# State-space stage of a sandwich kernel: one of two running sums of GpSimd handed to TensorE for part of the steps, softplus and gate tasks moved, decay factors in three PSUM banks

## The chip, the cores and the metric

One core of a Trainium2 chip runs the whole program. The metric is the device time of one execution in microseconds (us), median of three runs.

## The reference, cut to what matters

Two residual layers over 2 x 2048 tokens of width 256. The change touches only the first sublayer of the first layer, a Mamba block followed by a router:

```python
xm, z = jnp.split(x @ W_in.T, 2, axis=-1)          # x is RMS-normed
xc = silu(conv4(xm) + conv_b)
dt, Bm, Cm = jnp.split(xc @ W_xproj.T, [R, R + N], axis=-1)   # R = 64, N = 16
delta = softplus(dt @ W_dt.T + b_dt)
dA = exp(delta[..., None] * A)
dBx = delta[..., None] * Bm[:, :, None, :] * xc[..., None]
def step(h, t):                                     # over time, 16 states, 512 channels
    dA_t, dBx_t, C_t = t
    h = dA_t * h + dBx_t
    return (h, jnp.einsum('ben,bn->be', h, C_t))
y = (ys + D_skip * xc) * silu(z)
return y @ W_out.T
```

## The kernel before

The state-space stage is the function `mamba_phase`; routing, experts and the second layer follow it and are not touched. The work is cut into 8 **units**: two sequences (`hf` 0 and 1) times four blocks of 512 tokens, taken in turn, two units in one pass of a hardware loop (`NB` = 4 passes). A unit has 16 **steps** n = 0 to 15, one for each of the 16 states of the recurrence. The 512 channels lie on 128 partitions in four chunks c, and the 512 tokens are four tiles j of 128. All five engines run the steps, each in the order in which its program is written out, and meet at semaphores:

- **GpSimd (POOL)** at step n writes dBx of state n+1, as two `product` operations of 128x1024 (L396), and adds what ScalarE weighted for tiles 1 and 3 to the running sum `acc` (`add`, L408, 128x512). The order is product, add of tile 1, product, add of tile 3. At step 1 there is no addition (ScalarE starts the sum itself) but the small chain `front_power` (L373, L375). After step 13 stands `front_u` (L380), the product delta*xc of the next unit, and after step 14 `rms`, four small operations (L385 to L391).
- **VectorE (DVE)** scans state n in four chunks (`scan`, L779, 128x512), two chunks, then `summed` for tile 0 (L742: transposed state times C, added into `acc`), two chunks, then `summed` for tile 2. Between them lie the gating of y (steps 2 to 5), `softplus_fix`, `softplus_sub` and `softplus_add` (L683, L690, L697), two residual additions (L710), and statistics (L669, L716).
- **ScalarE (ACT)** at step n writes the decay factors exp(delta*A) of state n+1, one 128x512 chunk per PSUM bank (`factor`, L551; four banks `dA0` to `dA3`), and the weighted copies of tiles 1 and 3 (`weighted`, L565) into two buffers `part`. A factor of chunk c waits until the scan of chunk c of the state before has read that bank. Long tasks stand in two slots, MID_ACT and END_ACT, by step. `silus` (end of step 8) takes a table load, the silu of z (128x2048, L524), those of xc, and a load back.
- **TensorE (PE)** at step n transposes state n-1 into two banks `h_ps` (`turn`, L921, tiles 0, 1, then the tasks in EARLY, tiles 2, 3, then those in LATE). Tile 0 waits for VectorE to have read tile 2 before it, tile 1 for ScalarE to have read tile 3, and so on. The tasks are the projections of the next unit: `xc` (convolution as matmuls, L855), `dt` (L863), `d` (L868), `z` (L859), `o` (output, L874), the y of the unit before (L839, L841), the router `r` (L882). All data are float32.
- **SyncE (SP)** loads the B rows by DMA, three steps ahead.

Hence at step n the additions and transposes concern state n-1, the scan state n, the products and factors state n+1. The gate between GpSimd and TensorE is that a product of state n+1 needs all transposes of step n-2.

## Time and profile before

| | us |
|---|---|
| median of 3 runs | 2460.2 (2458.91 to 2461.51) |
| the profiled execution | 2457.92, of which span 2456.2 |
| period of one unit (GpSimd's `front_power` 222.34 to 352.02) | 129.68 |
| from step 1 of the first unit to step 1 of the last (92.63 to 1002.37) | 909.7 |

Busy over the whole span: TensorE 1920.1 us (78%), VectorE 1676.1 (68%), ScalarE 1185.9 (48%), GpSimd 1483.1 (60%). The stage ends at about 1150 us. Busy shares over the whole span say little here; what a change in the stage is worth is read within one unit. In the rows, L numbers are lines of the kernel; `a_dA`, `a_hs` and so on are its buffers with the stage's letter in front; "[3.42 <-ACT a_part L565]" means that the engine sat idle 3.42 us before this instruction, and that ScalarE's write of `part` ended it.

### The profile page before, as it was taken

What the parts mean: (1) busy time and instruction counts of PE and PEld (TensorE: products, weight loads), DVE (VectorE), ACT (ScalarE), POOL (GpSimd) and SP (SyncE); (2) the same over time, 40 slices, a digit from 0 to 9 for tenths busy, and PEclk for the clock granted to TensorE, in tenths of its full rate; (3) what the DMA queues carried; (4) which work ended last, traced back from release to release, by engine and by line L of the source; (5) the groups of instructions that cost most, each with busy time, mean ns of one, the idle gap of its engine ahead of it and who ended that gap; (6) DMA issues with size and microseconds to landing.
All of it is one profiled execution on the core that took longest, in us unless ns stands there. A gap on an engine that the chain in (4) does not pass through costs nothing. (4 is left out here: it accounts for less than half of the span.)

```text
span 2456.2 us, 35764 instructions
## 1 busy us (share of the span) xinstructions
PE 1920.1 (78%) x10252; PEld 1469.4 (60%) x10253; DVE 1676.1 (68%) x3193; ACT 1185.9 (48%) x2021; POOL 1483.1 (60%) x1118
## 2 busy tenths in 40 slices
PE   6787878796979787876599999907877784799970
PEld 2445454554555554644499999904655664699970
DVE  1789898989899898985644444436734897644438
ACT  2776767777777767773222222226632441111112
POOL 1799999898989898984133333335622420355532
PEclk9797979797989888887699999958987896799995
DMA  4111111111111010112411111142000014122226
GB/s 125 36 35 40 36 40 35 40 35 41 37 38 38 29 45 31 44 36 82 165 48 47 48 48 47 41 139 77 9 18 11 9 35 163 44 70 70 68 66 191
DMA packets 76781, 138.63 MB, mean 56 GB/s; under 512 B 10370, under 2 KB 47874, under 8 KB 75859
## 3 DMA queue, kind: packets, MB, share of 16 engines
q1 hardware_dynamic: 62994, 99.67, 12.3%
q0 software_dynamic: 13632, 37.24, 4.9%
q8 instruction: 56, 0.92, 0.2%
q14 instruction: 99, 0.80, 0.1%
HBM read 104.86 MB, written 32.01 MB: 56 GB/s over the span
## 5 line engine op out<-in xcount | busy, mean ns | idle before, releaser
L779 DVE TENSOR_TENSOR_SCAN a_hs<-a_dA,a_carry,a_hs 128x512 f32<-128x512 f32 x512 | 628.9, 1267 | 78.2 <-POOL a_hs L396 38.7
L396 POOL TENSOR_TENSOR a_hs<-a_u,a_b_bc 128x1024 f32<-128x1024 f32 x258 | 626.4, 2431 | 0.4
L921 PE MATMUL a_h_ps<-k_ident,a_hs 128*128 128x128 f32 x2064 | 326.6, 307 | 147.1 <-DVE a_acc L742 79.1
L921 PEld LDWEIGHTS a_h_ps<-k_ident,a_hs 128*128 128x128 f32 x2064 | 268.0, 158 | 270.8 <-DVE a_acc L742 75.5
L551 ACT ACTIVATE a_dA<-a_delta,a_a_neg 128x512 f32<-128x512 f32 x512 | 350.8, 688 | 31.2 <-DVE a_hs L779 29.3
L408 POOL TENSOR_TENSOR a_acc<-a_acc,a_part 128x512 f32<-128x512 f32 x242 | 317.7, 1313 | 59.7 <-ACT a_part L565 58.7
L565 ACT ACTIVATE a_part<-a_h_ps,a_c_tok 128x512 f32<-128x512 f32 x242 | 165.9, 686 | 193.6 <-PE a_h_ps L921 186.4
L1221 POOL DMA_INDIRECT expert_rows<-m0e_ys,k_pair x71 | 79.1, 1114 | 232.4 <-DVE m0e_ys L1277 217.9
L855 PE MATMUL a_fx<-a_hT,a_w_x 128*128 128x512 f32 x432 | 201.9, 599 | 2.2 <-ACT a_halo L487 1.4
L742 DVE SCALAR_TENSOR_TENSOR a_acc<-a_h_ps,a_c_tok,a_acc 128x512 f32<-128x512 f32 x242 | 176.1, 728 | 30.7 <-PE a_h_ps L921 30.7
L1287 DVE TENSOR_TENSOR m0e_hT<-m0e_gs,m0e_u 128x512 f32<-128x512 f32 x70 | 48.2, 689 | 190.9 <-ACT m0e_gs L1240 190.9
L1240 ACT ACTIVATE m0e_gs<-m0e_g 128x512 f32<-128x512 f32 x71 | 42.4, 597 | 269.6 <-PE m0e_u L1318 269.6
L1244 ACT ACTIVATE m1e_hT<-m1e_u 128x512 f32<-128x512 f32 x71 | 42.4, 597 | 226.3 <-PE m1e_u L1318 226.3
L1318 PE MATMUL m1e_u<-m1e_xT,m1e_wu 128*128 128x128 f32 x1136 | 140.2, 277 | 0.2 <-DVE m1e_wu L1271 0.2
L1318 PE MATMUL m0e_g<-m0e_xT,m0e_wg 128*128 128x128 f32 x1136 | 140.1, 277 | 0.0
L1267 DVE TENSOR_SCALAR m1e_xT<-m1e_x,k_ln_w,k_ln_b 128x128 f32<-128x128 f32 x142 | 51.8, 406 | 129.1 <-PE m1e_x L1306 129.0
L1318 PE MATMUL m0e_u<-m0e_xT,m0e_wu 128*128 128x128 f32 x1136 | 139.0, 276 | 0.0
L1328 PE MATMUL m0e_y<-m0w_down,m0e_hT 128*128 x568 | 134.5, 380 | 0.2 <-DVE m0e_ys L1277 0.2
L1318 PEld LDWEIGHTS m1e_u<-m1e_xT,m1e_wu 128*128 128x128 f32 x1136 | 134.1, 194 | 0.6 <-issue 0.5
L1318 PEld LDWEIGHTS m0e_g<-m0e_xT,m0e_wg 128*128 128x128 f32 x1136 | 134.2, 194 | 0.1
L1328 PE MATMUL m1e_y<-m1w_down,m1e_hT 128*128 x568 | 134.2, 379 | 0.0
L1221 POOL DMA_INDIRECT expert_rows<-m1e_ys,k_pair x71 | 70.0, 987 | 104.9 <-DVE m1e_ys L1277 89.0
(420 smaller groups left out, 3793.2 us busy)
## 6 DMA issues: line engine op xcount, KB each, us to landing
a_b_bc<-b_rows SPq DMA_DIRECT2D x132, 256.0 KB, 3.1
c_y<-expert_rows SPq DMA_DIRECT2D x16, 512.0 KB, 5.7
q_y<-expert_rows SPq DMA_DIRECT2D x16, 512.0 KB, 5.9
norm_rows<-a_x SPq DMA_DIRECT2D x9, 512.0 KB, 3.2
m0w_up<-in_m_up SPq DMA_DIRECT2D x1, 4096.0 KB, 12.5
m0w_gate<-in_m_gate SPq DMA_DIRECT2D x1, 4096.0 KB, 22.4
m0w_down<-in_m_down SPq DMA_DIRECT2D x1, 4096.0 KB, 31.9
c_xl<-in_L_attn_x SPq DMA_DIRECT2D x8, 512.0 KB, 3.5
```

The source lines that it names most:

```text
L396: pool.tensor_tensor(hs[n % NBUF][:, half, :], u[s][:, half, :], b_bc[:, n % NBUF:n % NBUF + 1, :].broadcast_to([P, 2, T]), ALU.mult).then ...
L408: pool.tensor_tensor(acc[s][:, j, :], acc[s][:, j, :], part[:, j // 2, :], ALU.add).then_inc(s_add, 1)
L551: act.activation(dA[c][:], delta[s][:, c, :], ACT.Exp, scale=a_neg[:, c, k:k + 1]).then_inc(s_da, 1)
L565: act.activation(to, hT_ps[j % 2][:], ACT.Copy, scale=c_tok[s][:, j, k:k + 1]).then_inc(s_part, 1)
L742: dve.scalar_tensor_tensor(out=acc[s][:, j, :], in0=hT_ps[j % 2][:], scalar=weight, in1=acc[s][:, j, :], op0=ALU.mult, op1=ALU.add).then_i ...
L779: dve.tensor_tensor_scan(hs[k][:, c, :], dA[c][:], hs[k][:, c, :], carry[:, hf, c, n:n + 1], ALU.mult, ALU.add).then_inc(s_scan, 1)
L855: last = pe.matmul(ps[:], w_x[:, q, d, k * P:(k + 1) * P], hT[:, d, q:q + T], start=q == 0 and d == 0, stop=q == KC - 1 and d == DC - 1)
L921: last = pe.transpose(hT_ps[j % 2][:, c * P:(c + 1) * P], hs[(n - 1) % NBUF][:, c, j * P:(j + 1) * P], ident[:])
L1221: pool.indirect_dma_start(io["expert_rows"], bass.IndirectOffsetOnAxis(ap=per.pair[:, s:s + 1], axis=0), ys[s % 2][:], None).then_inc(s_st ...
L1267: last = dve.tensor_scalar(xT[k][:, c, :], x_ps[:, c, :], scale[:, c:c + 1], shift[:, c:c + 1], ALU.mult, ALU.add)
L1318: last = pe.matmul(ps[k][:, f, :], w[k][:, c, f * P:(f + 1) * P], xT[k][:, c, :], start=c == 0, stop=c == DC - 1)
L1328: last = pe.matmul(y_ps[k][:], hT[k][:, c, :], w_down[:, c, bass.ds(e * D, D)], start=c == 0, stop=c == FC - 1)
```

## The change

- **Sum of tile 3.** For steps 9 to 15 and step 0 of the next unit, GpSimd no longer adds `part` of tile 3. TensorE adds it, as a matmul with the identity into a PSUM bank `sum` (`pile`), one step later, between transposes 1 and 2 (that of step 0 after transpose 3). At step 11 it adds what GpSimd had summed in steps 1 to 8 (`pile_acc`), and ScalarE copies the bank back at step 1 (`copy_sum`), before TensorE's first y task, which now waits for it. That is 9 matmuls for 8 additions in each unit.
- **Factors in three banks.** The bank comes from there: `dA` has three banks, used in turn. A factor now waits for the scan three chunks back, not four. `factor(n,3)` moves from the end of step n-1 to the start of step n, ahead of `weighted(n,1)`.
- **Tasks.** The silu of z goes from step 8 to a task of its own, `gates`, at the end of step 3. The `dt` projection is split over steps 9 and 10. Exponential, rounding and logarithm of the softplus each go half a step later. On VectorE `softplus_fix` goes from the middle to the end of step 12, `softplus_sub` from the end of step 12 to the middle of step 13, `softplus_add` from the middle to the end of step 13. `front_u` on GpSimd goes from after step 13 to after step 14.
- **RMS.** Three of the four small operations of `rms` go from GpSimd to VectorE as two. A buffer `part` is cleared in the prologue.

```diff
-        dA = [m.ps(f"dA{c}", [P, T]) for c in range(EC)]
+        RING = 3
+        dA = [m.ps(f"dA{c}", [P, T]) for c in range(RING)]
+        sum_ps = m.ps("sum", [P, ED])
+        last_y = dA + [sum_ps]
...
-                 11: ["d2", "d3"], 12: ["o0"], 13: ["z0"], 14: ["z3"], 15: ["r"]}
+                 10: ["dt.2", "dt.3"], 11: ["d2", "d3"], 12: ["o0"], 13: ["z0"], 14: ["z3"], 15: ["r"]}
...
-        MID_ACT = {1: ["norms"], 2: ["f1"], 10: ["dt"], 11: ["d2", "d3", "exp"], 13: ["z0"], 14: ["x1", "z2", "z3"]}
-        END_ACT = {0: ["moments"], 1: ["f0"], 4: ["xc0"], 5: ["own"], 6: ["xc1"], 7: ["xc2"], 8: ["silus"], 10: ["d0", "d1"],
-                   11: ["round", "ct"], 12: ["ln"], 13: ["z1"], 14: ["g0", "g1"], 15: ["rows"]}
+        MID_ACT = {1: ["norms"], 2: ["f1"], 10: ["dt"], 11: ["d2", "d3"], 12: ["round"], 13: ["z0", "ln"], 14: ["x1", "z2", "z3"]}
+        END_ACT = {0: ["moments"], 1: ["f0"], 3: ["gates"], 4: ["xc0"], 5: ["own"], 6: ["xc1"], 7: ["xc2"], 8: ["silus"], 10: ["d0", "d1"],
+                   11: ["exp", "ct"], 13: ["z1"], 14: ["g0", "g1"], 15: ["rows"]}
...
-        ND, NO, ADDS = len(ON), len(OFF), len(OFF) * (NS - 1)
+        LAST_ADD = 8
+        ADD_SEQ = [(0, 1)] + [(n, j) for n in range(2, NS) for j in OFF if j == 1 or n <= LAST_ADD]
+        PILE_SEQ = [(-1, 3), (0, 3)] + [(n, 3) for n in range(LAST_ADD + 1, NS - 1)]
+        PILE_SEQ.insert(4, ("acc", 3))
...
+        SLOT = [g % RING for g in range(NS * EC - 1)] + [1]
+
+        def slot(n, c):
+
+            return SLOT[(n * EC + c) % (NS * EC)]
+
+        def last_scan(n, c):
+
+            g = n * EC + c - 1
+            while SLOT[g % (NS * EC)] != slot(n, c):
+                g -= 1
+            return g
+
+        def piled(U, n):
+
+            return lin(U, PILES, PILE_SEQ.index((n, 3)) + 1)
...
+                pool.wait_ge(s_ms, nth)
...
-                        if n == 14:
-                            rms(tile0, lambda per_: lin(U, per_, per_))
-                        if n == NS - 3:
+                        if n == NS - 2:
                             pool.wait_ge(s_xc, lin(F, 1, 1))
                             pool.wait_ge(s_free[side("xc3")], count("xc3", U))
                             for q in range(2):
                                 front_u(F, 1 - hf, q)
+                        if n == 14:
+                            rms(tile0, lin(U, 1, 1))
             end = (0, 2 * NB, None)
...
-                act.wait_ge(s_scan, lin(U, NS * EC, (n - 1) * EC + c + 1 + SCANNED))
-                act.activation(dA[c][:], delta[s][:, c, :], ACT.Exp, scale=a_neg[:, c, k:k + 1]).then_inc(s_da, 1)
+                act.wait_ge(s_scan, lin(U, NS * EC, last_scan(n, c) + 1 + SCANNED))
+                act.activation(dA[slot(n, c)][:], delta[s][:, c, :], ACT.Exp, scale=a_neg[:, c, k:k + 1]).then_inc(s_da, 1)
+
+            def copy_sum(U, s):
+
+                act.wait_ge(s_sum, piled(U, 0))
+                act.activation(acc[s][:, 3, :], sum_ps[:], ACT.Copy).then_inc(s_sumc, 1)
 
             def weighted(U, n, j, s):
 
@@ -556,12 +581,16 @@
                     return
                 act.wait_ge(s_turn, turned(U, n, j))
                 k = (n - 1) % NS
+                to = part[:, j // 2, :]
                 if n == 1:
                     act.wait_ge(s_free[side("ct")], count("ct", before(U)))
                     to = acc[s][:, j, :]
+                elif j == 1:
+                    act.wait_ge(s_add, added_count(U, 0, 1) + -1 if n == 0 else added_count(U, n - 1 if n > 2 else 0, 1))
+                elif n == 2 or n == 0 or n > LAST_ADD + 1:
+                    act.wait_ge(s_sum, piled(U, n - 1 if n != 2 else 0))
                 else:
...
+                        factor(U, n, 3, hf)
                         weighted(U, n, 1, here)
+                        if n == 1:
+                            copy_sum(U, 1 - hf)
                         factor(U, n + 1, 0, there)
...
                         factor(U, n + 1, 2, there)
                         for name in END_ACT.get(n, []):
                             task(name)
-                        factor(U, n + 1, 3, there)
...
-                last.then_inc(s_mv2, 1)
+                link(last, padded=True)
+                link(dve.tensor_tensor(ms[:], mv2[:, :, 0], mv2[:, :, 0], ALU.mult))
+                dve.scalar_tensor_tensor(out=ms[:], in0=ms[:], scalar=EPS_RMS, in1=mv2[:, :, 1],
...
-                        if n == 12:
-                            softplus_fix(F, 1 - hf)
                         if n == 13:
-                            softplus_add(F, 1 - hf)
+                            softplus_sub(F, 1 - hf)
                         scan(2)
                         scan(3)
                         summed(U, n, 2, here)
                         summed(U, n, 3, here)
                         if n == 12:
-                            softplus_sub(F, 1 - hf)
+                            softplus_fix(F, 1 - hf)
                             dve.wait_ge(s_full["Y"], count("o0", U))
                             dve.wait_ge(s_xn, lin(U, 1, 1))
                             residual(0, fy, tile0).then_inc(s_free["Y"], 1)
+                        if n == 13:
+                            softplus_add(F, 1 - hf)
                         if n == 15:
                             dve.wait_ge(s_full["Y"], count("r", U))
...
+            def pile(U, n):
+
+                pe.wait_ge(s_part, part_count(U, n, 3))
+                if n == LAST_ADD + 1:
+                    pe.wait_ge(s_sumc, lin(U, 1, 1))
+                pe.matmul(sum_ps[:], ident[:], part[:, 1, :], start=n == LAST_ADD + 1, stop=n == 0).then_inc(s_sum, 1)
+
+            def pile_acc(U, s):
+
+                pe.wait_ge(s_add, added_count(U, LAST_ADD, 3))
+                pe.matmul(sum_ps[:], ident[:], acc[s][:, 3, :], start=False, stop=False).then_inc(s_sum, 1)
+
...
+                        if n == 0 or n > LAST_ADD + 1:
+                            pile(U, n - 1)
                         for name in EARLY.get(n, []):
                             task(name, U, F, 1 - hf)
                         turn(U, n, 2)
                         turn(U, n, 3)
+                        if n == 0:
+                            pile(U, 0)
+                        if n == LAST_ADD + 3:
+                            pile_acc(U, hf)
```

TensorE, the last transposes of step 9 to the first half of step 10, without the row numbers. The operand names are output<-inputs; `a_h_ps0` and `a_h_ps1` are the two transpose banks, L863/L900 is `dt`. Before:

```order
L863 MATMUL a_fy<-a_xc1,a_w_proj 96x512 x4
L915 REGISTER_ALU
L919 REGISTER_ALU
L921 MATMUL a_h_ps0<-k_ident,a_hs1 128x128 x4
L921 MATMUL a_h_ps1<-k_ident,a_hs1 128x128 x4
```

After:

```order
L900 MATMUL a_fy<-a_xc1,a_w_proj 96x512 x2
L953 REGISTER_ALU
L957 REGISTER_ALU
L959 MATMUL a_h_ps0<-k_ident,a_hs1 128x128 x4
L959 MATMUL a_h_ps1<-k_ident,a_hs1 128x128 x4
L967 MATMUL a_sum<-a_part,k_ident 128x512
L900 MATMUL a_fy<-a_xc1,a_w_proj 96x512 x2
```

Half of `dt` now stands behind the first transposes of step 10, with the first `pile` ahead of it.

VectorE, from `summed` of tile 0 of step 12 on. L683/L717 is `softplus_fix`, L690 is `softplus_sub`, L779/L816 the scans, L744 the first residual addition. Before:

```order
L742 SCALAR_TENSOR_TENSOR a_acc0<-a_h_ps0,a_c_tok0,a_acc0 128x512
L681 REGISTER_ALU
L683 SCALAR_TENSOR_TENSOR a_acc1<-a_acc1,a_u1 128x1024 x2
L777 REGISTER_ALU
L779 SCALAR_TENSOR_TENSOR a_hs0<-a_dA2,a_carry,a_hs0 128x512
L778 REGISTER_ALU
L779 SCALAR_TENSOR_TENSOR a_hs0<-a_dA3,a_carry,a_hs0 128x512
L733 REGISTER_ALU
L742 SCALAR_TENSOR_TENSOR a_acc0<-a_h_ps0,a_c_tok0,a_acc0 128x512
L689 REGISTER_ALU
L690 TENSOR_TENSOR a_delta1<-a_delta1,a_acc1 128x1024
```

After:

```order
L779 SCALAR_TENSOR_TENSOR a_acc0<-a_h_ps0,a_c_tok0,a_acc0 128x512
L814 REGISTER_ALU
L816 SCALAR_TENSOR_TENSOR a_hs0<-a_dA2,a_carry,a_hs0 128x512
L815 REGISTER_ALU
L816 SCALAR_TENSOR_TENSOR a_hs0<-a_dA0,a_carry,a_hs0 128x512
L770 REGISTER_ALU
L779 SCALAR_TENSOR_TENSOR a_acc0<-a_h_ps0,a_c_tok0,a_acc0 128x512
L715 REGISTER_ALU
L717 SCALAR_TENSOR_TENSOR a_acc1<-a_acc1,a_u1 128x1024 x2
L842 REGISTER_ALU
L744 ISA
L744 TENSOR_TENSOR k_hidden<-k_hidden,a_fy 128x512
```

The fix stands behind both scans and the second `summed` of the step, and the subtraction is no longer ahead of the residual addition.

ScalarE, the end of step 3 and the start of step 4. L551/L571 are factors, L565/L594 weighted copies, L542 is the silu of z. Before:

```order
L565 ACTIVATE a_part<-a_h_ps1,a_c_tok0 128x512
L550 REGISTER_ALU
L551 ACTIVATE a_dA2<-a_delta0,a_a_neg 128x512
L551 ACTIVATE a_dA3<-a_delta0,a_a_neg 128x512
L557 REGISTER_ALU
L563 REGISTER_ALU
L565 ACTIVATE a_part<-a_h_ps1,a_c_tok0 128x512
```

After:

```order
L594 ACTIVATE a_part<-a_h_ps1,a_c_tok0 128x512
L571 ACTIVATE a_dA0<-a_delta0,a_a_neg 128x512
L541 ISA
L541 REGISTER_ALU
L542 ACT_TABLE_LOAD
L542 ACTIVATE a_z0<-a_z0 128x2048
L570 REGISTER_ALU
L571 ACT_TABLE_LOAD
L571 ACTIVATE a_dA1<-a_delta0,a_a_neg 128x512
L582 REGISTER_ALU
L589 REGISTER_ALU
L594 ACTIVATE a_part<-a_h_ps1,a_c_tok0 128x512
```

Two table loads and the long silu now stand between a factor and the next, and ahead of the weighted copy of step 4.

## Rows read from the trace of the kernel before

**Rows 1.** Busy time by stretch: steps 1 to 8, 9 to 13, 14 to next step 1.
```profile
core 0: us, PE busy (x) PEld busy (x) DVE busy (x) ACT busy (x) POOL busy (x), PEclk, DMA share, GB/s
222.34:278.60 56.26, 52.90 (x242) 32.80 (x240) 51.30 (x53) 41.62 (x75) 56.16 (x34) 0.96 0.12 38
278.60:324.20 45.60, 33.80 (x130) 21.40 (x131) 38.05 (x34) 34.24 (x52) 38.37 (x21) 0.85 0.11 35
324.20:352.02 27.82, 17.09 (x88) 12.56 (x86) 25.52 (x43) 18.82 (x40) 27.49 (x20) 0.71 0.13 42
```
**Rows 2.** GpSimd in order of time: start, length, line, operation, idle before and its ender.
```profile
264.39 2.39 POOL L396 TENSOR_TENSOR a_hs<-a_u,a_b_bc 128x1024 f32<-128x1024 f32 x1
266.70 1.31 POOL L408 TENSOR_TENSOR a_acc<-a_acc,a_part 128x512 f32<-128x512 f32 x1
267.92 2.41 POOL L396 TENSOR_TENSOR a_hs<-a_u,a_b_bc 128x1024 f32<-128x1024 f32 x1
...
322.99 1.27 POOL L408 TENSOR_TENSOR a_acc<-a_acc,a_part 128x512 f32<-128x512 f32 x1 [3.42 <-ACT a_part L565]
324.21 4.69 POOL L380 TENSOR_TENSOR a_u<-a_delta,a_xc 128x1024 f32<-128x1024 f32 x2
...
336.90 1.02 POOL L391 TENSOR_TENSOR k_row_scale<-a_ms,a_halfneg 128x4 f32 x1 [0.17 <-POOL a_ms L389]
...
353.96 4.68 POOL L396 TENSOR_TENSOR a_hs<-a_u,a_b_bc 128x1024 f32<-128x1024 f32 x2
```
**Rows 3.** VectorE in order of time, step 9 to the next unit's step 2.
```profile
273.90 2.46 DVE L779 TENSOR_TENSOR_SCAN a_hs<-a_dA,a_carry,a_hs 128x512 f32<-128x512 f32 x2 [0.43 <-POOL a_hs L396]
...
280.54 1.28 DVE L779 TENSOR_TENSOR_SCAN a_hs<-a_dA,a_carry,a_hs 128x512 f32<-128x512 f32 x1 [1.80 <-ACT a_dA L551]
...
287.39 0.75 DVE L742 SCALAR_TENSOR_TENSOR a_acc<-a_h_ps,a_c_tok,a_acc 128x512 f32<-128x512 f32 x1 [2.56 <-PE a_h_ps L921]
...
300.46 1.28 DVE L779 TENSOR_TENSOR_SCAN a_hs<-a_dA,a_carry,a_hs 128x512 f32<-128x512 f32 x1 [2.10 <-ACT a_dA L551]
...
303.48 4.59 DVE L683 SCALAR_TENSOR_TENSOR a_acc<-a_acc,a_u 128x1024 f32<-128x1024 f32 x2 [1.09 <-ACT a_acc L539]
...
311.01 4.88 DVE L690 TENSOR_TENSOR a_delta<-a_delta,a_acc 128x1024 f32<-128x1024 f32 x2
...
341.44 2.46 DVE L779 TENSOR_TENSOR_SCAN a_hs<-a_dA,a_carry,a_hs 128x512 f32<-128x512 f32 x2 [2.21 <-issue]
...
356.35 2.46 DVE L779 TENSOR_TENSOR_SCAN a_hs<-a_dA,a_carry,a_hs 128x512 f32<-128x512 f32 x2 [1.07 <-POOL a_hs L396]
```
**Rows 4.** TensorE in order of time (a float32 matmul is two records).
```profile
250.61 3.60 PE L855 MATMUL a_fx<-a_hT,a_w_x 128*128 128x512 f32 x8
...
301.58 5.31 PE L874 MATMUL a_fy<-a_w_out,a_z 128*128 128x256 f32 x16
...
307.60 3.62 PE L874 MATMUL a_fx<-a_w_out,a_z 128*128 128x256 f32 x16
...
316.54 3.78 PE L859 MATMUL a_fy<-a_hT,a_w_z 128*128 128x512 f32 x4 [4.24 <-DVE k_hidden L710]
```
**Rows 5.** Busy time by stretch: steps 3 to 8, and steps 15 to 1 (columns as in Rows 1).
```profile
232.00:276.00 44.00, 43.47 (x195) 25.83 (x193) 41.76 (x43) 31.45 (x55) 44.00 (x26) 1.00 0.12 37
...
336.00:356.00 20.00, 11.66 (x44) 8.94 (x45) 17.02 (x26) 11.64 (x25) 19.57 (x16) 0.50 0.21 69
```
**Rows 6.** ScalarE in order of time: step 8's long task, step 1's `norms`.
```profile
272.88 1.28 ACT L524 ACT_TABLE_LOAD   x1
274.18 1.91 ACT L524 ACTIVATE a_z<-a_z 128x2048 f32<-128x2048 f32 x1
...
354.10 2.07 ACT L464 ACTIVATE a_hn<-k_hidden,a_nb,a_pw 128x256 f32 x4
```
**Rows 7.** VectorE in the prologue, GpSimd idle.
```profile
69.28 2.36 DVE L683 SCALAR_TENSOR_TENSOR a_acc<-a_acc,a_u 128x1024 f32<-128x1024 f32 x2 [53.51 <-ACT a_acc L539]
```
**Rows 8.** GpSimd's last addition of the state-space stage.
```profile
1126.76 1.26 POOL L408 TENSOR_TENSOR a_acc<-a_acc,a_part 128x512 f32<-128x512 f32 x1 [0.18 <-ACT a_part L565]
```

68 lines of the change are left out of this document (36 added, 32 removed).

## The prediction, made before the changed kernel was run

> **What bounds the kernel now.** I read first the busy time by stretch of one unit, 129.68 us long (a unit and a step are as defined with the kernel above). In steps 1 to 8 GpSimd is busy 56.16 of 56.26 us, and TensorE 52.90 at a clock of 0.96; in steps 9 to 13 no engine is full (VectorE 38.05 of 45.60); from step 14 to the next unit's step 1 GpSimd is full again, 27.49 of 27.82 [rows 1]. So the bound changes within a unit. Then GpSimd in order of time: it never idles from the `front_u` at 324.21 through the next unit's step 8. A product starts 2.31 us before the addition behind it, an addition 1.22 before the next product, so a step is 2 x (2.31 + 1.22) = 7.07 us [rows 2]. VectorE's own step is four scans of 1.2 (two take 2.46 [rows 3]) and two sums of 0.65 from start to start, 6.1 us, with 0.6 more in steps 2 to 5, where y is gated. Then VectorE in order of time, to see who is late where GpSimd isn't: a chain through ScalarE and TensorE. Between step 9's first scan (273.90) and the end of step 15's work (341.44 less the 2.21 of waiting, 339.23) it waits 0.45, 1.80, 2.56, 2.10 and 1.09, together 8.0 us of 65.3 [rows 3]. From there to step 2's first scan at 356.35 it takes 17.1 us, which GpSimd's chain sets.
>
> **The change, part by part, for one unit.** I follow each engine's queue from the rows' durations, with 0.1 us for a semaphore, over three stretches, and compare the moments at which VectorE begins step 9, step 0 and step 2.
>
> *GpSimd loses work.* Eight additions at 1.22 are 9.8 us, and three small operations of `rms`, on the engine that is full in two of three stretches. In the first stretch (steps 2 to 8) none goes, so 7.07 a step stays the pace there. TensorE needs 6.9 for these steps (a pair of transposes twice, and four matmuls of 128x512 at 0.86 to 0.9 each: 3.60 for four [rows 4]); it is busy 43.47 of 44 us at full clock [rows 5]. So even without GpSimd there would be little to win there, and a delay of TensorE would be paid.
>
> *Steps 9 to 15.* VectorE's work is 65.3 - 8.0 = 57.3 us, plus 0.5 for the two small operations of `rms` with their waits. I expect these waits:
> - Step 9: 0.45 for GpSimd as before. `silus` is shorter by z's 1.91 [rows 6], but starts one scan later, since the factor ahead of it now waits for the step's fourth scan: 1.0 instead of 1.80.
> - Step 10: only half of `dt` stands ahead of the transposes. The first sum waits 0.7 instead of 2.56, the second 0.5, since the other half of `dt` now stands ahead of it, and a `pile` with it.
> - Step 12: `exp` has left the place ahead of the factor, but d0 to d3 are late by the split `dt`: 1.3 instead of 2.10, then 0.9 for the fourth factor behind `exp`.
> - Step 12, o0: before, the fix (4.59 [rows 3]) lay on VectorE while TensorE ran o0. Now both scans and the second sum come first, and that sum's transposes stand behind o0, with a `pile` ahead of it: 1.0. The wait for the rounding (1.09) goes.
>
> The fix takes 2.36 us for both halves in the prologue, with GpSimd idle [rows 7], and 4.59 beside GpSimd's products; by my queue the products of the next states still run beside fix and subtraction, so I leave both at the price of before. The waits are 0.45 + 1.0 + 0.7 + 0.5 + 1.3 + 0.9 + 1.0 = 5.85 us, the stretch is 57.8 + 5.85 = 63.65: 1.65 us less. Nine `pile` matmuls at 0.86 (1.9 at half clock, 3.78 for two [rows 4]) otherwise fall where TensorE has room: it is busy 33.80 of 45.60 and 17.09 of 27.82 [rows 1].
>
> *Step 0 to step 2.* VectorE's own work is 7.85 (step 0 with its statistics) and 6.1: 13.95 us instead of 17.1, if GpSimd is not late. GpSimd's chain now starts from the addition of step 14: weighted copy, addition 1.2, product 2.3, `front_u` 4.7, power 1.0, product 2.3; the product for step 0 is there 13.0 us after step 14's first scan ends, and VectorE comes for it 13.4 after. Four tenths of room: VectorE sets the pace. That is 3.15 us more, together 4.8. At step 1 `copy_sum` (0.7, as a 128x512 copy) stands ahead of `norms` (2.07 [rows 6]) and step 2's second factor comes 0.8 late: 4.0 left.
>
> *Steps 2 to 8.* GpSimd enters ahead of VectorE and is then held twice by ScalarE. Its first addition of step 2 waits 1.2 for the weighted copy, which stands behind `norms` and a factor. In step 4 it waits 0.7 for `gates`: two table loads of 1.28 and 1.91 [rows 6] between the weighted copies. This stretch is bound by GpSimd, so it is paid where before it was part of one group in step 8; TensorE, held by the same copies, adds perhaps 0.3. The three banks cost nothing in an ordinary step: the factor's room is two scans and a sum, 3.0 us, less its 0.7. At the end of the stretch 4.0 + 0.9 (VectorE need not wait for GpSimd's first product) - 1.9 - 0.3 = 2.7; I take 3.0, since part of the 1.9 falls into each other.
>
> One sentence of the Trainium skill weighs against `gates`. The page "ScalarE: Activation LUTs" (section "What ACT_TABLE_LOAD costs") puts each switch of table at about 1.28 us plus a drain of 1.38, so the extra pair of switches would be 5.3 us and not 2.6. The rows show the load's 1.28 and the silu starting 1.30 after the start of the load [rows 6], without the drain; by the page the sum would be smaller by 2.7 us a unit.
>
> *The loop's turn.* After every second unit VectorE waits 2.21 us for nothing that the trace shows [rows 3]. Before, GpSimd's chain covered it (both kinds of unit last 129.7); now VectorE is the late one there, so at 3 of the 7 transitions about 2.1 of the 3.0 is not won.
>
> *Ends.* The first unit gains some 0.2, the last one its 1.65 of steps 9 to 15. At the very end, in place of an addition of 1.26 [rows 8], a `pile` (0.9 to 1.9) and a copy of 0.7 stand before the last y: 0.8 lost.
>
> **Sum.** 4 x 3.0 + 3 x 0.9 + 0.2 + 1.65 - 0.8 = 15.8 us. Against the profiled execution (2457.92, 2.3 below the median) that is 2442.2, against the median of 2460.2 it is 2444.4. I say **2444 us**. Bounds: if the new waits of steps 9 to 13 vanish (5.4) for all 8 units but TensorE's 6.9 a step still hold steps 2 to 8, about 40 us more could go, toward 2405; I hold that for unlikely, as each has a named cause. On the other side the half clock, below.
>
> **Rivals.**
> *(a) The relief arrives in full.* GpSimd with 9.8 us less runs further ahead, fix and subtraction meet it idle (2.2 and 2.4 less) and TensorE keeps full clock in steps 9 to 13. Then a unit gains 3.0 + 2.5: 2460 - 15.8 - 8 x 2.5 = 2424. For it: VectorE works only 51.3 + 38.1 + 25.5 = 114.9 of 129.7 us [rows 1]. Against it: by my queue GpSimd still writes the products of the next two states while the fix and the subtraction run.
> *(b) No gain: the three banks couple ScalarE to VectorE.* The factor of the next step's second chunk now waits for this step's third scan, and the weighted copy of tile 3 stands behind it. If this makes the copy late by 0.4 for GpSimd in each of the seven steps 2 to 8, 2.8 of the 3.0 us are gone: about 2459. For it: ScalarE, TensorE and GpSimd are all near full there. Against it: GpSimd waits for no copy in steps 2 to 8 now, so the copies have room.
> *(c) Slower: TensorE becomes the late engine from step 9 to 13.* In the stretch of steps 15 to 1 it runs at 0.50 of its clock, that is 1.2 of 2.4 GHz, after gaps of over 2 us [rows 5]; o0 took 5.31 after such a gap, o1 with the same work 3.62 [rows 4]. o0 is now uncovered, so half clock costs 1.7 there, 1.2 on the half of `dt`, and 1.0 on each of two `pile` ahead of transposes that are waited for: 4.9 a unit against 3.0, 1.9 slower, 2460 + 8 x 1.9 = 2475. It decides once the granted clock in steps 9 to 13 falls from 0.85 to under about 0.75.
> *(d) The table switches cost a drain at step 3 as well*, hidden in step 8 until now: 2.7 a unit on GpSimd's pace, 2444 + 22 = 2466. The page named above states such a drain.
>
> **Chances.** Forecast 0.52, (a) 0.20, (b) 0.14, (c) 0.10, (d) 0.04. A measurement of this kernel can tell about 0.2%, 5 us, from no change. Faster than 2455.3: the forecast and (a), 0.72. Within: (b), 0.14. Slower than 2465.1: (c) and (d), 0.14. The range for 8 in 10 takes in the forecast, (a) and (b): 2423 to 2462.
>
> **What will show it.** In the trace of the changed kernel the period from one `front_power` to the next should be 126 to 127 us inside a loop pass and about 129 across its turn. GpSimd should idle 8 to 10 us in steps 9 to 15, most of it for `part`. VectorE's waits for `dA` and the transposes should total about 6 us in a unit, with one behind o0. Step 4's first addition should wait for `part`. If instead VectorE waits for `part`'s chain in every one of steps 2 to 8, (b) holds; if the clock in steps 9 to 13 is under 0.75, (c); if GpSimd shows no idle time in steps 9 to 13, the relief was not delivered. My working is wrong first of all if a queue that I walked has one more wait, since 0.6 us in each unit is already 0.2%.

## The result: slower by 0.8%, and the profile after

The changed kernel takes **2478.6 us** (median of 4 runs, 2477.29 to 2480.15), against 2460.86 for the kernel before beside it (2458.91 to 2463.14). The ratio is 1.0077, 95% interval 1.0064 to 1.0089. 2444 us had been forecast, a gain of 16 us; it became a loss of 18. The profiled execution has a span of 2476.7 us, 20.5 above the one of before; the mean period from one `front_power` to the next is 132.6 us (92.0 to 1019.9), where it was 129.96.

The first view is the busy time of each engine in three stretches of the changed kernel. Columns: stretch, its length, busy time of TensorE's matmuls, its weight loads, VectorE, ScalarE and GpSimd, the granted clock, DMA share, GB/s. The stretches begin with the first scan of step 2, with the scan that answers to 273.90 of before, and with the end of step 15's work [rows 1, 3].

```profile
229.67:277.89 48.22, 45.87 (x215) 28.13 (x214) 45.30 (x47) 39.69 (x69) 46.04 (x27) 1.00 0.14 39
277.89:346.32 68.43, 50.81 (x222) 32.02 (x220) 62.90 (x64) 48.31 (x79) 53.66 (x27) 0.90 0.08 28
346.32:363.20 16.88, 12.05 (x44) 7.91 (x45) 13.69 (x21) 10.30 (x24) 12.36 (x8) 0.60 0.19 66
```

With before cut at the same instructions:

| | before | forecast | after |
|---|---|---|---|
| steps 2 to 8 | 47.2 | 49.0 (47.2 + 1.0, and 0.8 for `copy_sum`) | 48.2 |
| from step 9 to the end of step 15 | 65.3 | 63.65 | 68.4 (70.3 in the unit before) |
| from there to step 2, inside a pass | 17.1 | 13.95 | 13.8 |
| the same across the loop's turn | 17.1 | 16.05 (13.95 + 2.1) | 17.0 |

Three of the four rows came out within 1 us of the walk: the third to 0.2 us, steps 2 to 8 0.8 us shorter and the loop's turn 1 us longer. The loss is in the second one. So the next view is VectorE in order of time over that stretch, of the changed kernel (start, length, engine, line, operation, out<-in, count, and in brackets the idle time before and what ended it).

```profile
283.43 1.28 DVE L816 TENSOR_TENSOR_SCAN a_hs<-a_dA,a_carry,a_hs 128x512 f32<-128x512 f32 x1 [0.70 <-ACT a_dA L571]
...
288.59 0.75 DVE L779 SCALAR_TENSOR_TENSOR a_acc<-a_h_ps,a_c_tok,a_acc 128x512 f32<-128x512 f32 x1 [0.87 <-PE a_h_ps L959]
...
292.04 0.75 DVE L779 SCALAR_TENSOR_TENSOR a_acc<-a_h_ps,a_c_tok,a_acc 128x512 f32<-128x512 f32 x1 [0.34 <-PE a_h_ps L959]
...
298.77 0.75 DVE L779 SCALAR_TENSOR_TENSOR a_acc<-a_h_ps,a_c_tok,a_acc 128x512 f32<-128x512 f32 x1 [0.51 <-PE a_h_ps L959]
...
301.16 1.28 DVE L816 TENSOR_TENSOR_SCAN a_hs<-a_dA,a_carry,a_hs 128x512 f32<-128x512 f32 x1 [0.45 <-ACT a_dA L571]
...
304.87 1.28 DVE L816 TENSOR_TENSOR_SCAN a_hs<-a_dA,a_carry,a_hs 128x512 f32<-128x512 f32 x1 [0.59 <-ACT a_dA L571]
307.23 0.75 DVE L779 SCALAR_TENSOR_TENSOR a_acc<-a_h_ps,a_c_tok,a_acc 128x512 f32<-128x512 f32 x1 [1.08 <-PE a_h_ps L959]
307.98 5.58 DVE L717 SCALAR_TENSOR_TENSOR a_acc<-a_acc,a_u 128x1024 f32<-128x1024 f32 x2
...
332.59 1.78 DVE L757 TENSOR_TENSOR a_ms<-a_mv 128x4 f32<-128x4 f32 x1
...
334.41 2.26 DVE L758 SCALAR_TENSOR_TENSOR a_ms<-a_ms,a_mv 128x4 f32<-128x4 f32 x1
...
345.47 0.75 DVE L779 SCALAR_TENSOR_TENSOR a_acc<-a_h_ps,a_c_tok,a_acc 128x512 f32<-128x512 f32 x1 [0.41 <-PE a_h_ps L959]
...
349.19 2.46 DVE L816 TENSOR_TENSOR_SCAN a_hs<-a_dA,a_carry,a_hs 128x512 f32<-128x512 f32 x2 [2.87 <-issue]
```

With the 0.45 before them, the waits up to 307.23 are 4.99 us; 5.85 had been forecast for the stretch. What was not forecast are durations. `softplus_fix` takes 5.58 us (4.59 before [rows 3]), and the two small RMS operations, of 128x4 elements, take 1.78 and 2.26 us and were put down at 0.5 together.

What GpSimd does at those moments, in the same kernel:

```profile
306.83 5.66 POOL L414 TENSOR_TENSOR a_hs<-a_u,a_b_bc 128x1024 f32<-128x1024 f32 x2
...
332.00 2.36 POOL L414 TENSOR_TENSOR a_hs<-a_u,a_b_bc 128x1024 f32<-128x1024 f32 x1
334.30 4.65 POOL L404 TENSOR_TENSOR a_u<-a_delta,a_xc 128x1024 f32<-128x1024 f32 x2
```

The first small operation, begun at 332.59, ends at 334.37; GpSimd's product ends at 334.36. The second ends at 336.67, when the first of the two `front_u` operations (4.65 for both) is over. All 8 units are alike in this; the ninth execution stands behind the loop. The view of all executions of one line gives minimum, median and maximum in ns:

```profile
L757 DVE TENSOR_TENSOR a_ms<-a_mv x9: 157/1498/1790, 200.2 to 1170.9; 128x4 f32<-128x4 f32 x9
```

```profile
L758 DVE SCALAR_TENSOR_TENSOR a_ms<-a_ms,a_mv x9: 164/2261/2265, 201.8 to 1171.1; 128x4 f32<-128x4 f32 x9
```

The minimum, 157 and 164 ns, is that of the execution behind the loop, where no `front_u` follows and GpSimd is idle. The second consequence lies on TensorE. In time order, first TensorE in the first unit of a pass, then VectorE:

```profile
207.16 1.97 PE L959 MATMUL a_h_ps<-k_ident,a_hs 128*128 128x128 f32 x8 [5.60 <-DVE a_acc L779]
...
210.62 3.42 PE L919 MATMUL a_fy<-a_w_router,a_acc 128*128 128x8 f32 x16
```

```profile
215.03 0.75 DVE L779 SCALAR_TENSOR_TENSOR a_acc<-a_h_ps,a_c_tok,a_acc 128x512 f32<-128x512 f32 x1 [2.63 <-PE a_h_ps L959]
```

TensorE idles 5.60 us while VectorE stands in the two operations, and then takes 3.42 us for the router. That is the lower of its two clock levels: the same router takes 1.85 at the upper one, as below. VectorE pays with a wait of 2.63 us for transposes, at a place where it had none. Not every unit goes this way. The next one has a longer gap, and the router runs at the upper level:

```profile
339.81 1.97 PE L959 MATMUL a_h_ps<-k_ident,a_hs 128*128 128x128 f32 x8 [5.88 <-DVE a_acc L779]
...
343.10 1.85 PE L919 MATMUL a_fy<-a_w_router,a_acc 128*128 128x8 f32 x16
```

In this trace the router takes 3.42 us in four of the eight units (2.6 us of waiting each on VectorE) and 1.85 to 1.87 in the other four (0.3 to 0.6 each), after gaps of 5.6 to 5.9 us in all eight. Together VectorE waits 12.3 us at this place.

### The profile page after: what moved, and what is told of

Its sections match the earlier page's. It is cut to its first block and busy times, and to the rows that moved or that the text cites. A ratio compares the mean times of both kernels' runs of the same rounds, so it can differ in the third digit from the quotient of the medians.

```text
span 2476.7 us, 35927 instructions
## 1 busy us (share of the span) xinstructions
PE 1944.3 (79%) x10402; PEld 1468.3 (59%) x10403; DVE 1720.4 (69%) x3220; ACT 1210.6 (49%) x2045; POOL 1397.8 (56%) x1026
## 5 line engine op out<-in xcount | busy, mean ns | idle before, releaser
L816 DVE TENSOR_TENSOR_SCAN a_hs<-a_dA,a_carry,a_hs 128x512 f32<-128x512 f32 x512 | 631.9, 1268 | 53.2 <-POOL a_hs L414 26.2
L571 ACT ACTIVATE a_dA<-a_delta,a_a_neg 128x512 f32<-128x512 f32 x512 | 352.8, 689 | 206.7 <-DVE a_hs L816 205.3
L959 PEld LDWEIGHTS a_h_ps<-k_ident,a_hs 128*128 128x128 f32 x2064 | 262.2, 154 | 278.3 <-DVE a_hs L816 95.2
L959 PE MATMUL a_h_ps<-k_ident,a_hs 128*128 128x128 f32 x2064 | 314.6, 297 | 141.4 <-DVE a_acc L779 100.2
L426 POOL TENSOR_TENSOR a_acc<-a_acc,a_part 128x512 f32<-128x512 f32 x177 | 227.9, 1288 | 158.4 <-ACT a_part L594 158.4
L779 DVE SCALAR_TENSOR_TENSOR a_acc<-a_h_ps,a_c_tok,a_acc 128x512 f32<-128x512 f32 x242 | 176.8, 730 | 40.3 <-PE a_h_ps L959 40.1
L594 ACT ACTIVATE a_part<-a_h_ps,a_c_tok 128x512 f32<-128x512 f32 x242 | 164.0, 678 | 45.6 <-PE a_h_ps L959 45.1
L1348 DVE TENSOR_TENSOR m0e_hT<-m0e_gs,m0e_u 128x512 f32<-128x512 f32 x70 | 48.2, 688 | 190.5 <-ACT m0e_gs L1301 190.5
L1379 PE MATMUL m0e_u<-m0e_xT,m0e_wu 128*128 128x128 f32 x1136 | 138.6, 275 | 0.0
L1379 PEld LDWEIGHTS m0e_u<-m0e_xT,m0e_wu 128*128 128x128 f32 x1136 | 132.8, 192 | 0.0
```

The lines of the kernel that those rows point to most:

```text
L426: pool.tensor_tensor(acc[s][:, j, :], acc[s][:, j, :], part[:, j // 2, :], ALU.add).then_inc(s_add, 1)
L571: act.activation(dA[slot(n, c)][:], delta[s][:, c, :], ACT.Exp, scale=a_neg[:, c, k:k + 1]).then_inc(s_da, 1)
L594: act.activation(to, hT_ps[j % 2][:], ACT.Copy, scale=c_tok[s][:, j, k:k + 1]).then_inc(s_part, 1)
L779: dve.scalar_tensor_tensor(out=acc[s][:, j, :], in0=hT_ps[j % 2][:], scalar=weight, in1=acc[s][:, j, :], op0=ALU.mult, op1=ALU.add).then_i ...
L816: dve.tensor_tensor_scan(hs[k][:, c, :], dA[slot(n, c)][:], hs[k][:, c, :], carry[:, hf, c, n:n + 1], ALU.mult, ALU.add).then_inc(s_scan, 1)
L959: last = pe.transpose(hT_ps[j % 2][:, c * P:(c + 1) * P], hs[(n - 1) % NBUF][:, c, j * P:(j + 1) * P], ident[:])
```

## The experiments

Each median stands beside a median of the kernel before on the same chip. Since the kernel before took 2457.15 to 2461.48 us in these groups, kernels of different groups are compared by their ratios to it; a difference of ratios is turned into us with 2460.

Two theories came first. **L**: the small operations on VectorE wait for GpSimd's running operation, and that, with what follows, is the loss. **T**: the loss comes from the rest of the change (three banks, `gates`, matmuls that add, softplus order).

**1. The small RMS operations back on GpSimd, all else as changed.**

```diff
+                pool.tensor_tensor(ms[:], mv2[:, :, 0], mv2[:, :, 0], ALU.mult).then_inc(s_ms, 1)
+                pool.tensor_tensor(ms[:], ms[:], eps_rms[:], ALU.add).then_inc(s_ms, 1)
+                pool.tensor_tensor(ms[:], ms[:], mv2[:, :, 1], ALU.add).then_inc(s_ms, 1)
...
-                link(dve.tensor_tensor(ms[:], mv2[:, :, 0], mv2[:, :, 0], ALU.mult))
-                dve.scalar_tensor_tensor(out=ms[:], in0=ms[:], scalar=EPS_RMS, in1=mv2[:, :, 1],
```

> The changed kernel with one part undone: the three small RMS operations (square of the mean, eps, variance, 128x4) are again GpSimd's, not two of VectorE's. Theory L (lock): in the changed kernel these two VectorE operations read two SBUF operands each and took 1.64 and 2.26 us on average where they took 0.16 each at the very end, with GpSimd idle, because each waits for the GpSimd operation that runs; that is 3.7 us a unit on VectorE, which is the late engine there, 29 us in all, and the TensorE clock that falls in the gap behind it. It expects 2446 to 2453 us, and VectorE's step 14 to be some 4 us shorter. Theory T (TensorE): the loss is from the sum on TensorE and the uncovered output projection at step 12. It expects 2474 to 2480 us, since nothing of that changes.

Measured: 2438.37 us (2436.87 to 2445.53), ratio 0.9932 (0.9912 to 0.9952). L holds and T falls: without this one part the change is a gain of 17 us, more than L's 2446 to 2453 us had allowed for. Beside number 10, which differs from it by less than the intervals, it is the fastest kernel of the study. GpSimd does the same work in three operations of 0.2 us each. TensorE there, in the first unit of a pass:

```profile
204.56 1.09 PE L965 MATMUL a_h_ps<-k_ident,a_hs 128*128 128x128 f32 x8 [1.74 <-DVE a_acc L785]
...
206.35 1.85 PE L925 MATMUL a_fy<-a_w_router,a_acc 128*128 128x8 f32 x16
```

The gap is 1.74 us and not 5.60, and the router takes 1.85. What VectorE does at the end of that unit:

```profile
211.90 2.46 DVE L822 TENSOR_TENSOR_SCAN a_hs<-a_dA,a_carry,a_hs 128x512 f32<-128x512 f32 x2 [1.35 <-POOL a_hs L423]
```

Here it waits 1.35 us for GpSimd's product at step 0. So not all that the two operations cost comes back: VectorE comes 4 us sooner, and GpSimd does the three small operations again ahead of that product.

**2. The same operations on VectorE, but ahead of step 14's scans.**

```diff
                         dve.wait_ge(s_carry, lin(U, NS, n + 2))
+                        if n == 14:
+                            dve.wait_ge(s_free["X"], count("o1", U))
+                            rms_stats(tile0, lin(U, 1, 1))
...
                         scan(0)
...
-                        if n == 14:
-                            dve.wait_ge(s_free["X"], count("o1", U))
-                            rms_stats(tile0, lin(U, 1, 1))
```

> The changed kernel with the same instructions, but VectorE's statistics and the two small RMS operations stand ahead of the scans of step 14, not between its two pairs of scans. There GpSimd sat idle for 5.8 to 6.1 us, waiting for a weighted copy that itself waits for the first scan. Theory L: each of the two operations takes 0.16 to 0.2 us, and the time is 2446 to 2453 us. Theory T: 2474 to 2480 us. If the two operations are slow by their own nature on VectorE (small tiles, dependence), they keep 1.6 and 2.3 us and the time stays at 2478 too.

Measured: 2451.01 us (2446.42 to 2457.97), ratio 0.9976 (0.9962 to 0.9989). All executions of the first small operation, and then GpSimd's waits between 90 and 1150 us (total, times, longest):

```profile
L757 DVE TENSOR_TENSOR a_ms<-a_mv x9: 156/158/158, 196.1 to 1140.4; 128x4 f32<-128x4 f32 x9
```

```profile
POOL a_acc L426 <- ACT a_part L594: 138.6, 48, 8.3
```

At a moment when GpSimd idles (from 191.23 to 199.22 in the unit where it stands at 196.09), the same instruction takes 0.158 us, and so in every unit. That is theory L in one line: operands, engine and code are the same, and what runs on GpSimd differs. The kernel is still 11 us behind number 1. A likely cause is that the statistics now stand ahead of the scans, and with them everything that GpSimd's chain waits for (its waits are 138.6 us, and 118.3 in number 1); this was not tested by itself.

**3. The kernel before with the small operations on VectorE alone.**

```diff
-                pool.tensor_tensor(ms[:], mv2[:, :, 0], mv2[:, :, 0], ALU.mult).then_inc(s_ms, 1)
...
+                link(dve.tensor_tensor(ms[:], mv2[:, :, 0], mv2[:, :, 0], ALU.mult))
```

> The kernel before with only one part of the change: the three small RMS operations of GpSimd become two of VectorE. Theory L: they take 1 to 2.4 us each here too, since GpSimd is always busy there, but VectorE had 3.3 us of waiting for GpSimd between this place and step 2, and GpSimd is relieved of 0.96 us: 2453 to 2464 us, so the same two operations that cost 29 us in the changed kernel cost nothing here. Theory T: 0.2 us each, 2452 to 2460 us; the durations tell the two apart, not the time.

Measured: 2471.33 us (2470.5 to 2474.75), ratio 1.0055 (1.0038 to 1.0072): slower, above what I had expected. VectorE, then GpSimd:

```profile
200.63 1.01 DVE L717 TENSOR_TENSOR a_ms<-a_mv 128x4 f32<-128x4 f32 x1
...
201.68 1.19 DVE L718 SCALAR_TENSOR_TENSOR a_ms<-a_ms,a_mv 128x4 f32<-128x4 f32 x1
...
212.17 0.75 DVE L739 SCALAR_TENSOR_TENSOR a_acc<-a_h_ps,a_c_tok,a_acc 128x512 f32<-128x512 f32 x1 [0.92 <-PE a_h_ps L918]
```

```profile
199.26 2.36 POOL L390 TENSOR_TENSOR a_hs<-a_u,a_b_bc 128x1024 f32<-128x1024 f32 x1
201.58 1.26 POOL L402 TENSOR_TENSOR a_acc<-a_acc,a_part 128x512 f32<-128x512 f32 x1
```

The first operation ends at 201.64 and the product at 201.62; the second at 202.87 and the addition at 202.84. Here they cost 2.2 us and not 4.0, since a short addition stands behind the product and not `front_u`. What I had missed is that the transposes are late behind them here too: 0.92 behind a router of 3.42 us, and 1.34 at 230.46, behind matmuls for y most of which also ran at the lower clock. The router takes 3.42 us in all eight units here, and in four of eight in the kernel before.

**4. The changed kernel with z's silu back in step 8.**

```diff
-                act.activation(z[s][:], z[s][:], ACT.Silu).then_inc(s_zc, 1)
...
+                act.activation(z[1 - s][:], z[1 - s][:], ACT.Silu).then_inc(s_zc, 1)
```

> The changed kernel with the silu of z back in the long task at the end of step 8 (one pair of table loads a unit, not two). If a table switch costs a drain or the task at step 3 holds GpSimd's chain by more than the 1.0 us for which its addition waits in the trace, the time falls by 10 us or more, to under 2469. By the prediction's own step (0.7 us of GpSimd's time won at step 4, but the long task at step 8 1.9 us longer, with VectorE waiting for it) it stays within 2472 to 2486.

Measured: 2493.2 us (2490.99 to 2494.87), ratio 1.0145 (1.0128 to 1.0162). So the move of `gates` is worth 17 us, in spite of its extra pair of table loads. One row of VectorE shows why:

```profile
285.08 1.28 DVE L817 TENSOR_TENSOR_SCAN a_hs<-a_dA,a_carry,a_hs 128x512 f32<-128x512 f32 x1 [2.49 <-ACT a_dA L572]
```

With three banks, VectorE waits 2.49 us for a factor behind the full `silus`, and 0.70 without z's part. 1.8 us in each of 8 units are 14 us, and over the stage VectorE's waits for factors rise by 11.5 (29.9 for 18.4); what the rest of the 17 us is was not traced. The time lies above the whole range expected: the prediction's step had `gates` about neutral.

**5. The kernel before with three banks alone** (slots, waits and the fourth factor's place at the start of the next step as in the change; no other part of it).

```diff
-                act.wait_ge(s_scan, lin(U, NS * EC, (n - 1) * EC + c + 1 + SCANNED))
+                act.wait_ge(s_scan, lin(U, NS * EC, last_scan(n, c) + 1 + SCANNED))
```

> The kernel before with one part of the change alone: the decay factors use three PSUM banks in turn (the fourth lies unused), the fourth factor stands at the start of the next step. By the prediction's step (room of 3.0 us for a factor in an ordinary step, a little lost at the long tasks of steps 8 and 11) the time is 0 to 8 us above before, ratio 1.000 to 1.003. Rival (b), ScalarE coupled to VectorE in every step, expects 16 us or more above, ratio 1.007 and up.

Measured: 2506.98 us (2503.51 to 2511.7), ratio 1.0192 (1.0175 to 1.0209), 47 us slower: the largest effect of the study, and "the three banks cost nothing in an ordinary step" had been my line. VectorE, then GpSimd:

```profile
287.69 1.28 DVE L793 TENSOR_TENSOR_SCAN a_hs<-a_dA,a_carry,a_hs 128x512 f32<-128x512 f32 x1 [2.49 <-ACT a_dA L565]
...
295.69 0.75 DVE L756 SCALAR_TENSOR_TENSOR a_acc<-a_h_ps,a_c_tok,a_acc 128x512 f32<-128x512 f32 x1 [3.71 <-PE a_h_ps L935]
...
319.31 5.39 DVE L704 TENSOR_TENSOR a_delta<-a_delta,a_acc 128x1024 f32<-128x1024 f32 x2
...
328.83 4.79 DVE L711 TENSOR_TENSOR a_delta<-a_delta,a_u 128x1024 f32<-128x1024 f32 x2
```

```profile
327.98 1.27 POOL L422 TENSOR_TENSOR a_acc<-a_acc,a_part 128x512 f32<-128x512 f32 x1 [4.36 <-ACT a_part L579]
329.21 3.33 POOL L410 TENSOR_TENSOR a_hs<-a_u,a_b_bc 128x1024 f32<-128x1024 f32 x1
```

In steps 2 to 8 VectorE has no wait that before had not, so the line is right as it stands; the time is in the range that rival (b) had claimed, but not by its mechanism. But each long task meets VectorE with one scan less in hand: 2.49 for 1.80, 3.71 for 2.56 [rows 3]. After the subtraction the chain goes on: ScalarE waits for a scan behind the long VectorE operations, its weighted copy comes 4.36 us late for GpSimd, GpSimd's product (3.33) now runs beside `softplus_add`, and this takes 4.79 us where it took 2.35.

**6. Twice the adding matmuls.** Number 1 with each of the 8 matmuls that add `part` issued twice.

```diff
-                pe.matmul(sum_ps[:], ident[:], part[:, 1, :], start=n == LAST_ADD + 1, stop=n == 0).then_inc(s_sum, 1)
+                pe.matmul(sum_ps[:], ident[:], part[:, 1, :], start=n == LAST_ADD + 1, stop=False)
+                pe.matmul(sum_ps[:], ident[:], part[:, 1, :], start=False, stop=n == 0).then_inc(s_sum, 1)
```

> The kernel with RMS back on GpSimd (label e1_rms_gpsimd, ratio 0.993 to before), and each of the eight matmuls that add a weighted copy in a unit issued twice (so the sum of tile 3 for those steps counts double: part of the computation is changed): 64 more matmuls of 128x512, 0.86 us each at full clock, 55 us of TensorE. If they lie where TensorE has room, as the prediction said, the time rises by under 6 us, ratio under 0.996. If they stand ahead of transposes for which VectorE waits (it waits for transposes 38 times, 28.6 us in all, in e1), each such one is paid: 4 a unit by 0.86 us, 27 us, ratio 1.004.

Measured: 2454.2 us (2449.87 to 2461.21), ratio 0.9983 (0.9971 to 0.9995), 13 us above number 1. That lies between the two forecasts. 64 more matmuls cost 0.2 us each, a quarter of the 0.86 that one takes. They don't all fall where TensorE has room: VectorE's waits for transposes rise from 30.2 to 59.0 us (90 to 1150 us), and in part take the place of its waits for factors (12.3 for 18.8).

**7. The small operations in a form with one tensor operand**, at the place of the changed kernel.

```diff
-                link(dve.tensor_tensor(ms[:], mv2[:, :, 0], mv2[:, :, 0], ALU.mult))
+                for j in range(TJ):
+                    last = dve.tensor_scalar(ms[:, j:j + 1], mv2[:, j, 0:1], mv2[:, j, 0:1], mv2[:, j, 1:2], ALU.mult, ALU.add)
+                link(last)
+                dve.tensor_scalar(ms[:], ms[:], EPS_RMS, None, ALU.add).then_inc(s_ms, 1)
```

> The changed kernel with the RMS operations on VectorE at the same place, but in a form with one tensor operand in SBUF: four tensor_scalar of 128x1 with the mean and the variance as per-partition scalars, then one of 128x4 that adds eps. Theory L (the wait is for the second SBUF read path, shared with GpSimd): each takes under 0.2 us, the time is near that of e1, ratio 0.992 to 0.997. If any VectorE operation on this tile waits for GpSimd, whatever its operands, they keep over 1 us and the ratio stays at 1.007.

Measured: 2469.4 us (2462.53 to 2471.95), ratio 1.0039 (1.0026 to 1.0052): 9 us better than the change, and far from number 1, so between the two forecasts. VectorE, GpSimd, then TensorE:

```profile
198.32 0.27 DVE L758 TENSOR_SCALAR a_ms<-a_mv 128x1 f32<-128x1 f32 x1
...
199.17 0.65 DVE L760 TENSOR_SCALAR a_ms<-a_ms 128x4 f32<-128x4 f32 x1
...
210.82 0.75 DVE L780 SCALAR_TENSOR_TENSOR a_acc<-a_h_ps,a_c_tok,a_acc 128x512 f32<-128x512 f32 x1 [2.62 <-PE a_h_ps L960]
```

```profile
197.45 2.35 POOL L414 TENSOR_TENSOR a_hs<-a_u,a_b_bc 128x1024 f32<-128x1024 f32 x1
```

```profile
202.96 1.96 PE L960 MATMUL a_h_ps<-k_ident,a_hs 128*128 128x128 f32 x8 [3.29 <-DVE a_acc L780]
...
206.42 3.42 PE L920 MATMUL a_fy<-a_w_router,a_acc 128*128 128x8 f32 x16
```

The four operations with one tensor operand and per-partition scalars take 0.27 each and wait for nobody, though GpSimd's product runs. The last one, a scalar added to 128x4, took 0.65 here and 0.95 in the next unit, and 0.17 behind the loop with GpSimd idle. It ends at 199.82 and 330.23, and GpSimd's product ends at 199.80 and 330.21: it too waits for GpSimd, with a single tensor operand. So two SBUF operands are not what it takes; whether the form of 128x1 is spared by its single column or by its per-partition scalars was not tried. The whole tail is now 1.5 to 1.8 us long, over 2 less than in the changed kernel, some 18 us over 8 units. Yet the gap of TensorE is 3.29 us, the router takes 3.42, and VectorE waits the same 2.62. The router does so in seven of the eight units (gaps of 3.3 to 3.6 us) and not in four, so VectorE waits 16.9 us at this place and not 12.3; at the loop's turns it loses another 3.8 (12.3 for 8.5). That leaves about 9.

That raised a second question. **C**: what remains is TensorE's clock, which falls in the gap. **R**: the clock is not the point, the transposes are only late in the queue. The test is to put work into the gap that waits for nothing and changes nothing: matmuls that multiply by zeros.

**8. Ten such matmuls at the end of step 14 in the changed kernel.**

```diff
+                        if n == 14:
+                            for q in range(10):
+                                pe.matmul(sum_ps[:, 0:D], nil[:], w_out[:, q % EC, :], start=False, stop=False)
```

> The changed kernel with ten matmuls of 256 columns added at the end of step 14's tasks on TensorE. They multiply by zeros and add into the open bank of the sum, so they change no number and wait for nothing. In the changed kernel TensorE idles 5.6 us there while VectorE is held in its two small RMS operations, then runs the router at half clock (3.42 us), and VectorE waits 2.6 us for the transposes behind it. Theory C (the idle gap lowers the clock, and that is the rest of what the two small operations cost): the fillers cover 4.4 us of the gap, the router takes 1.9 us, VectorE's wait of 2.6 shrinks to under 0.6, and the time falls by 15 to 20 us to about 2460; the small operations keep their 4 us. Rival R (the transposes are late because everything behind the router is late, not because of the clock): the time stays within 3 us of 2478.6, or rises by what the fillers take.

Measured: 2456.97 us (2453.26 to 2458.79), ratio 0.9984 (0.9974 to 0.9994), 23 us less than the change. TensorE, then VectorE's waits between 90 and 1150 us, of this kernel and of the changed one:

```profile
201.82 4.48 PE L1004 MATMUL a_sum<-a_w_out,a_nil 128*128 128x256 f32 x20
207.59 1.09 PE L961 MATMUL a_h_ps<-k_ident,a_hs 128*128 128x128 f32 x8 [1.29 <-DVE a_acc L781]
...
209.38 1.85 PE L921 MATMUL a_fy<-a_w_router,a_acc 128*128 128x8 f32 x16
```

```profile
DVE a_acc L781 <- PE a_h_ps L961: 20.5, 24, 2.1
```

```profile
DVE a_acc L779 <- PE a_h_ps L959: 38.3, 42, 2.6
```

The router takes 1.85 us in all eight units, VectorE's waits behind it are gone (12.3 us in the changed kernel), and its waits for transposes fall by 17.8 us in all. The small operations keep their 1.50 and 2.27. Adding work to TensorE has made the kernel faster.

**9. Five of them in number 7.** The edit is that of number 8 with `range(5)`.

> The kernel with the small RMS operations on VectorE as operations with one tensor input (2469.4 before this edit), with five such zero matmuls at the end of step 14: its gap on TensorE was 3.3 us, the router 3.42 us, VectorE's wait 2.6 us in one kind of unit and 1.8 in the other. Theory C: the waits go, 8 times about 2 us, less what GpSimd then makes VectorE wait at step 0 (1.3 where it was seen): about 2455, from 2448 to 2460. Rival R: 2466 to 2475.

Measured: 2452.47 us (2448.13 to 2455.57), ratio 0.9966 (0.9952 to 0.9979), 18 us less than without them. C again: the router takes 1.85 us in all eight units, and the 16.9 us of waits at this place are gone.

**10. Three of them in number 1, as a control** (`range(3)`).

> Control: the changed kernel with the small RMS operations back on GpSimd (2438.4) plus three of the zero matmuls at the end of step 14. There TensorE's gap was 1.7 us and the router ran at full clock (1.85 us) without fillers. Theory C: nothing is left to win there, so the time stays at 2438, within 4 us. If it falls by more than 5 us, the fillers do something other than keep the clock up at step 15, and C is not what the other two runs show.

Measured: 2443.41 us (2437.32 to 2443.5), ratio 0.9925 (0.9908 to 0.9942), against 0.9932 without them. By the ratio nothing is gained, as C says: there the router had run at the upper level in seven of eight units (2.10 us in the eighth), and VectorE had waited 2.25 us in all behind it. The median alone lies 5 us higher, but so does that of the kernel before in this group.

**11. Number 1 with the old places of the softplus on VectorE** (`softplus_fix` in the middle of step 12, `softplus_sub` at its end).

```diff
+                        if n == 12:
+                            softplus_fix(F, 1 - hf)
                         scan(2)
```

> The kernel with RMS back on GpSimd (e1, ratio 0.993), with VectorE's softplus fix in the middle of step 12 and the subtraction at its end again, as before the change; the final addition stays at the end of step 13. By the prediction the new order uncovers the output projection (1.0 us a unit) and saves the wait for the rounding (1.1): within 5 us of e1, ratio 0.991 to 0.995. If the new order is a loss, because transposes stand behind the projection with nothing to do on VectorE, this kernel is 8 us or more faster than e1, ratio under 0.990.

Measured: 2459.82 us (2455.69 to 2463.33), ratio 1.0001 (0.999 to 1.0012), 17 us above number 1, and outside both forecasts. VectorE:

```profile
304.98 5.57 DVE L726 SCALAR_TENSOR_TENSOR a_acc<-a_acc,a_u 128x1024 f32<-128x1024 f32 x2 [4.89 <-ACT a_acc L568]
```

The rounding on ScalarE now comes half a step later, so the fix at its old place waits 4.89 us for it.

## Why the prediction was wrong, step by step

**The step that failed** is the first line under "Steps 9 to 15": "plus 0.5 for the two small operations of `rms` with their waits". I had taken the price from the size of the operation (0.2 us each on GpSimd) and forgotten what I had just used for `softplus_fix`: such a VectorE operation is not independent of GpSimd. They take 4.04 us in the unit shown and 3.76 in the one before. Over the stage's 8 units the two lines are busy 13.1 + 18.1 = 31.2 us, where 4.0 stood in the sum; at 0.16 each they would be 2.6, so **28.6 us are waiting**. The Trainium skill's page "SBUF — State Buffer" describes in its section "Who interferes with whom" a port pair that VectorE and GpSimd share under an exclusive lock. By that rule a VectorE operation waits for the end of GpSimd's running one, and the traces agree to 0.1 us in the four pairs read here, the changed kernel's and number 3's. Number 7 shows the same for an operation of one tensor operand.

**What I had named as rival (c)** came true in another place. TensorE's clock fell, not in steps 9 to 13 but at step 15, in the gap that the small operations open (granted clock 0.86 in the first unit's stretch from step 9, 0.92 in number 1's). From step 9 to 13 it was 0.96 (277.89 to 325.40), where (c) needed under 0.75. Between 90 and 1150 us the books are: number 1 saves the 31.2 us, and 9.7 of waits for transposes (28.6 for 38.3); it loses 4.2 to GpSimd, which is next late (25.6 for 21.4). That makes 36.7, and the ratios say 36. Number 1's ratio gives 2443 us on 2460, the forecast for the whole change; that is luck, since the fix is 8 us dearer than in the sum and other terms came out cheaper. Filling the gap instead saves 23 us in the changed kernel and 18 in number 7, more than those 9.7. It also takes away waits for transposes that number 1 keeps (20.5 us in number 8, 28.6 in number 1).

**Waits of steps 9 to 13.** By number: 0.45 forecast and 0.45 measured, 1.0 and 0.70, 0.7 and 0.87, 0.5 and 0.34, 1.3 and 0.51 + 0.45, 0.9 and 0.59, 1.0 and 1.08 behind o0; another 0.41 at step 15. Together 5.85 and 5.40. The 0.51 stands behind transposes of step 11 and had not been named. Walking the queues gave these waits right to 0.4 us each. In the unit before, the last one is 2.63 for 0.41 behind the slow router, 7.6 in all.

**`softplus_fix` at the price of before** was 1.0 us too low: it takes 5.58, as two products run beside it for its whole length and not one for half of it. The subtraction (4.82) and the addition (2.35) kept theirs. So the stretch is 68.4 for 63.65: 3.5 for the small operations, 1.0 for the fix, -0.45 for the waits; 0.7 I can't assign.

**Steps 0 to 2** were right for a pass (13.8 for 13.95), but there VectorE had lost 4 us on the way. The 0.4 us of room that I gave GpSimd goes in number 1, where VectorE waits 1.35 for it: VectorE does none of the small operations there and GpSimd 0.9 us more. With the short ones of number 9, GpSimd's product ends at 208.97 and VectorE comes at 210.10, without a wait.

**Steps 2 to 8** became 1.0 us longer, where the sum has 1.8: the two waits of GpSimd came as walked, but the 0.8 for `copy_sum` ahead of step 2's second factor shows as a wait of 0.26 and 0.21. GpSimd, the changed kernel:

```profile
234.23 1.27 POOL L426 TENSOR_TENSOR a_acc<-a_acc,a_part 128x512 f32<-128x512 f32 x1 [1.20 <-ACT a_part L594]
...
249.45 1.27 POOL L426 TENSOR_TENSOR a_acc<-a_acc,a_part 128x512 f32<-128x512 f32 x1 [0.97 <-ACT a_part L594]
```

1.2 had been forecast at step 2 and came as 1.20, 0.7 at step 4 and came as 0.97.

**Rival (a)** needed GpSimd idle beside fix and subtraction. GpSimd idles 14.8 us in steps 9 to 15 of the unit shown, where 8 to 10 had been forecast, so it was relieved. But its products still run beside both (5.58 and 4.82 us).

**The three banks** cost nothing in an ordinary step, and 47 us if the long tasks stay where they were (number 5). **The moves of tasks**, which I had booked as 1.0 for 1.80 at step 9 and some tenths around the softplus, are what pays that back: 17 us for `gates` (number 4), 17 us for the place of fix and subtraction once their inputs have moved (number 11). I had priced each part against the kernel before and never against the change less that part, so none of these three sizes stood in the sum.

**The loop's turn.** The wait that the trace puts to nothing became 2.87 us (2.21 before), so hardly anything of the unit's gain is won across it, as forecast.

**Rival (d)**, the drain at a table switch, is refuted by number 4's 17 us of gain. ScalarE in the changed kernel, at `gates`:

```profile
243.47 1.28 ACT L542 ACT_TABLE_LOAD   x1
244.76 1.92 ACT L542 ACTIVATE a_z<-a_z 128x2048 f32<-128x2048 f32 x1
246.70 1.28 ACT L571 ACT_TABLE_LOAD   x1
247.99 0.69 ACT L571 ACTIVATE a_dA<-a_delta,a_a_neg 128x512 f32<-128x512 f32 x1
```

From the first load to the factor are 4.52 us, two loads of 1.28 and a silu of 1.92 with nothing between them. The section "What ACT_TABLE_LOAD costs" of the Trainium skill's page "ScalarE: Activation LUTs" adds a drain of 1.38 to each; the measurement decides against it here. **Rival (b)** fell as well: in steps 2 to 8 GpSimd waits for a copy only at the two places above, and VectorE waits 18.4 us in the whole stage for factors and 32.0 before.

## What to carry to other kernels

Price an operation that you move to VectorE by what GpSimd runs at that moment, not by its size: here it lasted until GpSimd's current operation ended, though it was 4 elements wide, with two SBUF operands and in one form with a single one. Before you call a stall small, look which engine idles behind it and whether TensorE comes out of the gap at the lower clock, in every unit and not in one; VectorE waited 12 us behind that here, and filling the gap won 23. And test the parts of a bundled change against the bundle less that part, since three banks lose 47 us alone and two moves of tasks are worth 17 each, and the total shows none of it.

## What the runs showed of the hardware

- A VectorE operation of 128x4 on two SBUF operands takes 0.16 us with GpSimd idle, and 1.0 to 2.3 us with GpSimd at work, ending within 0.1 us of GpSimd's operation. With one tensor operand of 128x4 and an immediate scalar it takes 0.17 with GpSimd idle and 0.65 to 0.95 beside it, and ends with GpSimd's operation too. With one of 128x1 and per-partition scalars it takes 0.27 in both cases.
- Matmuls that compute nothing made the kernel faster by 23 us (number 8).
- The gap's length alone does not decide at which level TensorE runs behind it. The router took 3.42 us in four of eight units of the kernel before (gaps of 2.2 us), in four of eight of the changed one (5.6 to 5.9), in seven of eight in number 7 (3.3 to 3.6) and in all eight in number 3 (3.8 to 4.6). After gaps of at most 1.74 us (numbers 1, 8, 9 and 10) it took 1.85, once 2.10. In the changed kernel's unit with the router at 1.85 behind a gap of 5.88, the transposes ahead of it still ran slow (1.97 us for eight, 1.09 at the upper level). What decides was not tried.
- What VectorE waits for at the loop's turn stays open (2.2 us before, 2.9 in the changed kernel, up to 4.3 in number 7); no run was made for it. In numbers 8 and 9 the trace names GpSimd's product there (waits of 1.96 and 2.97 us), but this had ended 5.5 and 4.2 us before the scan began.
